# A decoder's second cross attention: where the layernorm behind its output projection is worked

## The chip, the cores and the metric

The kernel runs on 1 core of one Trainium2 chip. The metric is the time of one execution on the device in microseconds (us), less is better; three runs of the kernel before gave 1655.15, 1655.97 and 1658.78 us, median 1655.97.

## The reference

Two pre-norm decoder layers over x of 8 sequences x 112 tokens x 512, in float32. Each layer is self attention, cross attention to a context, and a feed-forward part:

```
x = x + _L1_xattn_ref(_layernorm(x, axis=-1), ctx_512, L1_xattn_Wq, L1_xattn_Wkv_expand, L1_xattn_Wout)
x = x + _L1_ffn_ref(_layernorm(x, axis=-1), L1_ffn_Wg, ..., L1_ffn_bsd)
```

The change lies between these two lines of the second layer. The cross attention has 16 heads of 32 with a causal mask over 112 keys, softmax, and the projection Wout (512 x 512). The layernorm that follows takes each token's mean and variance over 512 values, subtracts and divides by sqrt(var + 1e-5). The feed-forward part is a mixture of experts: two rounds, each with a gate, six routed experts and a shared part.

## The kernel before, in words

The program is written by hand: every stage has one function for each engine (pe_ for TensorE, act_ for ScalarE, dve_ for VectorE, pool_ for GpSimd), each engine works its list strictly in that order, and semaphores named by engine and step join them. So the order of the lines is the order of the work; there is no planner.

The 896 tokens (8 x 112) are held as NT = 7 tiles of 128 in x. A matrix product keeps float32 accuracy with three matmuls: each operand is split into a rounded high part and the rest, the low part (mm3, lines 261 to 263). For a normalised tile this is: transposing by TensorE into one PSUM bank in four pieces (ln_turn, line 266), a copy by ScalarE that rounds it, the high part (ln_hi, line 338), and a subtraction by VectorE, the low part (ln_lo, line 342).

pe_att2, act_att2, dve_att2 and pool_att2 are the cross attention, one sequence a wave, w from 0 to NB + 1 = 9. Wave w computes the scores of sequence w (banks 0 to 3), and turns and applies the probabilities of earlier ones: a sequence has two groups of heads, so group 15 is the last one. power is the exponential, sum8 and share8 the softmax's sum and division, turn8 and turned the transposing of the probabilities (banks 4, 5) and their copy, values the product with V (bank 6), hi and lo its high and low part (line 2002 and 2046). Bank 7 (FILL) takes what is done beside: from wave 5 to 8 the output tiles 0 to 3 (output2, 12 matmuls of 128x512), which dve_att2 adds to x (residual, line 768) and takes the statistics of (stats2, lines 2088 and 2090).

pe_o2, act_o2 and dve_o2 follow: output tiles 4, 5, 6, and the layernorm of all seven. root2 (line 2102) is the square root on ScalarE; norm2 the reciprocal (line 2095) and the scaling into RES (line 2097); RES lies over the keys K2. pe_o2 ends with a wait for the low part of tile 3, behind which pe_moe begins with up(0, 0): 24 matmuls of 128x448 that read tiles 0 to 3. Then it turns tile 6 (which waits for tile 4's low part), does the gate's products and goes on.

The weights come as a stream of pieces through three buffers stg: a DMA by SyncE, the rounding copy on ScalarE (round_w, line 302), the rest on GpSimd (rest_w, line 307). A buffer is loaded again once its rest is done. first_up is the first piece of the experts; the two behind it are copied in act_o2 behind tile 3's high part, and need that TensorE is done with output tile 6, whose weights lie in their place.

Of the kernel before, what the change touches and what calls it, by code (L numbers as in the profile page):

```python
# [14 lines left out]
NB, S, D, L = 8, 112, 512, 375  # L15
T = NB * S
P, NT = 128, NB * S // 128
# [58 lines left out]
def build(nc, g):  # L76
# [8 lines left out]
    with ExitStack() as ctx:  # L85
# [1812 lines left out]
        def pe_att2(e):  # L1898
            def scores(w):
                for i in range(4):  # L1900
                    if w:
                        e.wait_ge(*upon("act_a2", "exp", 2 * w - 2 + i // 2))
                    e.matmul(PS[0:S, i, 0:HT], one[0:S, 0:S], maskR[:, :].unsqueeze(1).to_broadcast([S, 4, S]), start=True,
                             stop=True)
                for c in range(4):
                    for i in range(4):
                        p = slice(32 * i, 32 * i + 32)
                        last = e.matmul(PS[0:S, i, c * S:(c + 1) * S], QO[p, 1 + 2 * w, c, :], K2[p, c, w * S:(w + 1) * S],
                                        start=False, stop=True, skip_group_check=True)
                        if c == 3:  # L1910
                            last.then_inc(*done("pe_a2", "sc", w, i))

            def less(u):
                e.wait_ge(*upon("dve_a2", "mx", u))
                for i in range(2):
                    last = e.matmul(PS[0:S, 2 * (u % 2) + i, 0:HT], one[0:S, 0:S], r4(nmr[:, u % 4, 4 * i:4 * i + 4], S),
                                    start=False, stop=True, skip_group_check=True)
                last.then_inc(*done("pe_a2", "sub", u))

            def values(w):  # L1920
                e.wait_ge(*upon("act_a2", "pt", 2 * w + 1))
                e.wait_ge(*(upon("dve_a2", "lo", w - 1) if w else upon("dve_ln", "ln2", NT - 1, "lo")))
                for c in range(4):
                    for i in range(4):
                        last = e.matmul(PS[32 * i:32 * i + 32, 6, c * S:(c + 1) * S],
                                        V2[:, w, 128 * c + 32 * i:128 * c + 32 * i + 32], PT[i // 2][:, 4 * (i % 2) + c, :],
                                        start=True, stop=True)
                last.then_inc(*done("pe_a2", "pv", w))

            def ahead(w):  # L1930
                if w < 4:
                    if w:
                        e.wait_ge(*upon("dve_q2", "v" if w == 3 else "k", *((2,) if w == 3 else (w - 1, 1))))
                    else:
                        e.wait_ge(*upon("act_q2", 1))
                        e.wait_ge(*upon("dve_ln", "ln2", NT - 1, "lo"))
                    query2(e, 4 + w, FILL)
                elif 4 < w < 9:
                    e.wait_ge(*upon("dve_q2", "v", w - 1))
                    output2(e, w - 5, FILL)  # L1940

            def between(w):
                if w < 4:
                    e.wait_ge(*upon("act_q2", 4 + w))
                    key2(e, w, 1, FILL)
                elif w == 4:
                    e.wait_ge(*upon("dve_q2", "v", 3))
                    value2(e, 4, FILL)
                elif w < 8:
                    e.wait_ge(*upon("dve_o2", "x", w - 5))  # L1950
                    value2(e, w, FILL)

            def behind(w):
                if w in (2, 3):
                    e.wait_ge(*upon("dve_q2", "k", w, 1))
                    value2(e, w, FILL)

            e.wait_ge(*upon("dve_q2", "v", 1))
            e.wait_ge(*upon("act_a2", "mask"))
            e.wait_ge(*upon("act_q2", 3))  # L1960
            for w in range(NB + 2):
                if w == 4:
                    e.wait_ge(*upon("act_q2", 7))
                    e.wait_ge(*upon("dve_q2", "k", 3, 1))
                if w < NB:
                    scores(w)
                if w > 1:
                    turn8(e, "a2", 2 * w - 3)
                ahead(w)
                if w < NB:  # L1970
                    less(2 * w)
                if w > 1:
                    e.wait_ge(*upon("dve_q2", "v", w - 2))
                    values(w - 2)
                between(w)
                if w < NB:
                    less(2 * w + 1)
                if 0 < w <= NB:
                    turn8(e, "a2", 2 * w - 2)
                behind(w)  # L1980
# [4 lines left out]
        def act_att2(e):  # L1985
            def power(u):
                if u > 3:
                    e.wait_ge(*upon("pe_a2", "tr", u - 4))
                e.wait_ge(*upon("pe_a2", "sub", u))
                e.activation(Sb[u % 4][:, :, :].rearrange("p (i j) s -> p i j s", i=2), pairv(2 * (u % 2)), ACT.Exp,  # L1990
                             scale=float(np.float32(1.0) / np.sqrt(np.float32(32.0)))).then_inc(*done("act_a2", "exp", u))

            def turned(u):
                if u > 1:
                    e.wait_ge(*upon("pe_a2", "pv", u // 2 - 1))
                e.wait_ge(*upon("pe_a2", "tr", u))
                e.activation(PT[u % 2][:, :, :].rearrange("p (i j) s -> p i j s", i=2), pairv(4),
                             ACT.Copy).then_inc(*done("act_a2", "pt", u))

            def hi(w):  # L2000
                e.wait_ge(*upon("pe_a2", "pv", w))
                e.activation(parts2(0, w), psv(6), ACT.Copy).then_inc(*done("act_a2", "hi", w))

            e.wait_ge(*upon("pe_ln", "ln2", NT - 1))
            e.activation(maskR[:, :], C("mask1", S), ACT.Copy).then_inc(*done("act_a2", "mask"))
            for w in range(NB + 2):
                if w > 1:
                    turned(2 * w - 3)
                if w < 4:
                    query2_out(e, 4 + w, FILL)  # L2010
                if w < NB:
                    power(2 * w)
                if w > 1:
                    hi(w - 2)
                if w < NB:
                    power(2 * w + 1)
                if 0 < w <= NB:
                    turned(2 * w - 2)
                if w in (2, 4):
                    round_w(e, piece["o2", w // 2 - 1][0])  # L2020
                if w == NB:
                    round_w(e, first_up)

        def dve_att2(e):
# [5 lines left out]
            for w in range(NB + 2):  # L2030
# [13 lines left out]
                if w > 1:  # L2044
                    e.wait_ge(*upon("act_a2", "hi", w - 2))
                    e.tensor_tensor(parts2(1, w - 2), psv(6), parts2(0, w - 2).bitcast(F),
                                    A.subtract).then_inc(*done("dve_a2", "lo", w - 2))
                if 4 < w < 9:
                    stats2(e, w - 5)
                if w < NB:  # L2050
                    sum8(e, "a2", 2 * w)
                if w in (2, 3):
# [51 lines left out]
        def pe_o2(e):  # L2104
            for t in range(4, NT):
# [1 line left out]
                if t == 4:  # L2107
                    e.wait_ge(*upon("act_a2", "pt", 2 * NB - 1))
                output2(e, t, t)
                if t > 4:  # L2110
                    ln_turn(e, "lne", t - 5, RES[:, t - 5, :], t - 5)
            for t in range(2, NT - 1):
                ln_turn(e, "lne", t, RES[:, t, :], t)
            e.wait_ge(*upon("dve_ln", "lne", 3, "lo"))

        def act_o2(e):
            for t in range(4):
                root2(e, t)
            root2(e, 4)
            ln_hi(e, "lne", 0, 0)  # L2120
            root2(e, 5)
            ln_hi(e, "lne", 1, 1)
            root2(e, 6)
            for t in range(2, NT - 1):
                ln_hi(e, "lne", t, t)
                if t == 3:
                    for k in (1, 2):
                        round_w(e, first_up + k)

        def dve_o2(e):  # L2130
            e.wait_ge(*upon("pe_a2", "sc", NB - 1, 3))
            norm2(e, 0)
            residual(e, "o2", 4)
            stats2(e, 4)
            norm2(e, 1)
            residual(e, "o2", 5)
            stats2(e, 5)
            ln_lo(e, "lne", 0, 0)
            norm2(e, 2)
            residual(e, "o2", 6)  # L2140
            stats2(e, 6)
            ln_lo(e, "lne", 1, 1)
            for t in range(3, NT):
                norm2(e, t)
                ln_lo(e, "lne", t - 1, t - 1)

        def pool_o2(e):
            for k in (1, 2):
# [649 lines left out]
```

## Time and profile before

| | |
|---|---|
| median of 3 runs | 1655.97 us |
| the profiled execution | 1654.79 us |
| its span | 1652.9 us |
| busy: PE, DVE, ACT, POOL | 96%, 57%, 44%, 40% |
| chain that ended last: PE, DVE, ACT, issue | 84%, 7%, 4%, 4% |
| mean granted TensorE clock | 0.992 |

A view of the profile lists instructions by start, duration, engine and source line; "idle before" is how long the engine had nothing, and the arrow says what ended it. The chain of waits is followed back from the last instruction of the program to what released each step. Times are us from the start of the span. The granted clock (PEclk) is a share of the full 2.4 GHz; 0.50 is 1.2 GHz. The execution's time is 1.89 us more than its span.

### The profile page before, as it was taken

To read this page: it belongs to the slowest core of one execution; us is meant where nothing else is said; L and a number is where in the kernel's file an instruction comes from. 1 tells how busy PE (TensorE), PEld (TensorE's weight loads), DVE (VectorE), ACT (ScalarE), POOL (GpSimd) and SP (SyncE) were. 2 spreads that over 40 slices of the span, in tenths; PEclk is the share of its full clock that TensorE was granted. 3 is DMA by queue.
4 is the path that set the end of the run, shared out by engine and by line. 5 is a ranking of instruction groups with operands and counts; after the bars stand their busy time and mean duration, and the time that the engine had idled before them with its cause. 6 is when DMAs were issued, how large, how long until landed. Compare 5 with 4: busy or idle time off the path is not lost.

```text
span 1652.9 us, 24562 instructions
## 1 busy us (share of the span) xinstructions
PE 1589.1 (96%) x9832; PEld 1353.0 (82%) x9832; DVE 939.1 (57%) x1531; ACT 733.0 (44%) x1231; POOL 665.8 (40%) x483
## 2 busy tenths in 40 slices
PE   7999999999999999989999989998989999999998
PEld 7998666778899998768889976877768888888887
DVE  6555663366545555687668566353766455554554
ACT  3113654322587765665511156333545334353342
POOL 3875542540498873421137633212422422222321
PEclk9999999999999999999999999999999999999999
DMA  4110003123222007200001100110011111111111
GB/s 166 52 64 28 2 2 121 50 85 128 93 88 64 14 2 266 93 1 1 1 13 64 52 26 2 48 39 26 20 33 39 45 64 45 51 46 51 51 58 45
DMA packets 28581, 88.52 MB, mean 54 GB/s; under 512 B 4155, under 2 KB 4283, under 8 KB 28216
## 3 DMA queue, kind: packets, MB, share of 16 engines
q1 hardware_dynamic: 28468, 86.96, 15.7%
q8 instruction: 79, 1.29, 0.3%
q14 instruction: 34, 0.27, 0.1%
HBM read 85.11 MB, written 1.84 MB: 53 GB/s over the span
## 4 chain that ended last, share of the span: by engine, by line
PE 84%; DVE 7%; ACT 4%; issue 4%; POOL 1%; DMA 0%; SPq 0%; ACTq 0%; DVEq 0%; POOLq 0%
PE PS L261 19%; PE PS L263 18%; PE PS L262 18%; PE PS L266 7%; PE PS L1125 4%; PE PS L1462 3%; PE PS L1477 2%; PE PS L561 2%; PE PS L952 1%; PE PS L585 1%; PE PS L1709 1%; PE PS L1697 1%; PE PS L551 1%; PE PS L569 1%; DVE xn L326 1%
## 5 line engine op out<-in xcount | busy, mean ns | idle before, releaser
L307 POOL TENSOR_TENSOR HL<-stg,HL 128x1024 fp32r<-128x1024 f32 (+2 forms) x111 | 243.9, 2200 | 515.8 <-ACT HL L302 497.7
L261 PE MATMUL PS<-XT,HL 128*128 128x448 f32 x608 | 226.1, 372 | 2.9 <-DVE XT L342 2.2
L263 PE MATMUL PS<-XT,HL 128*128 128x448 f32 x608 | 223.8, 368 | 0.0
L262 PE MATMUL PS<-XT,HL 128*128 128x448 f32 x608 | 223.7, 368 | 0.0
L302 ACT ACTIVATE HL<-stg 128x1024 fp32r<-128x1024 f32 (+2 forms) x111 | 104.5, 944 | 215.1 <-PE PS L263 199.1
L261 PE MATMUL PS<-HL,XT 128*128 128x512 f32 (+1 forms) x380 | 138.3, 364 | 2.0 <-POOL HL L307 1.2
L262 PE MATMUL PS<-HL,XT 128*128 128x512 f32 (+1 forms) x380 | 135.5, 356 | 0.0
L263 PE MATMUL PS<-HL,XT 128*128 128x512 f32 (+1 forms) x380 | 135.4, 356 | 0.0
L261 PEld LDWEIGHTS PS<-XT,HL 128*128 128x128 f32 x608 | 115.6, 190 | 15.2 <-DVE XT L342 3.3
L262 PEld LDWEIGHTS PS<-XT,HL 128*128 128x128 f32 x608 | 115.7, 190 | 9.3
L263 PEld LDWEIGHTS PS<-XT,HL 128*128 128x128 f32 x608 | 115.3, 190 | 9.4
L1076 POOL TENSOR_TENSOR Sx<-Sx,rx 112x750 f32<-112x750 f32 x64 | 91.8, 1440 | 54.0 <-DVE rx L1178 53.9
L2416 DVE SCALAR_TENSOR_TENSOR Hh<-PS,sml,Hh 128x448 fp32r<-128x448 f32 x64 | 43.8, 684 | 119.2 <-ACT Hh L2302 119.2
L261 PE MATMUL PS<-HL,Ph 128*128 128x512 f32 x224 | 90.4, 404 | 2.7 <-DVE ACC L2448 0.9
L725 DVE TENSOR_TENSOR XT<-QO,XT 128x896 fp32r<-128x896 f32 x32 | 36.8, 1159 | 98.4 <-ACT XT L719 98.4
L1738 POOL TENSOR_TENSOR Sb<-Sb,rc 112x896 f32<-112x896 f32 x32 | 53.7, 1685 | 94.3 <-DVE rc L1733 94.2
L2302 ACT ACTIVATE Hh<-PS,sml 128x448 fp32r<-128x448 f32 x64 | 40.6, 635 | 109.1 <-PE PS L263 109.1
L263 PE MATMUL PS<-HL,Ph 128*128 128x512 f32 x224 | 87.6, 391 | 0.0
L262 PE MATMUL PS<-HL,Ph 128*128 128x512 f32 x224 | 87.5, 391 | 0.0
L1125 PE MATMUL PS<-PX,kvr 125*128 125x224 f32 x384 | 84.2, 355 | 0.0
L261 PEld LDWEIGHTS PS<-HL,XT 128*128 128x128 f32 (+1 forms) x380 | 70.8, 186 | 14.1 <-issue 1.9
L1097 DVE TENSOR_REDUCE nm<-PS 112x2 f32<-112x750 f32 x64 | 60.1, 939 | 38.3 <-PE PS L263 38.3
(314 smaller groups left out, 3808.6 us busy)
## 6 DMA issues: line engine op xcount, KB each, us to landing
stg<-in_wst SPq DMA_DIRECT2D x87, 512.0 KB, 3.3
stg<-in_wst SPq DMA_DIRECT2D x16, 352.0 KB, 3.1
stg<-in_wst SPq DMA_DIRECT2D x16, 320.0 KB, 3.3
wsum<-in_wfc SPq DMA_DIRECT2D x8, 512.0 KB, 3.7
wsum<-in_wpj SPq DMA_DIRECT2D x8, 512.0 KB, 3.5
raw<-in_wfc SPq DMA_DIRECT2D x8, 512.0 KB, 7.5
stg<-in_wst SPq DMA_DIRECT2D x16, 256.0 KB, 2.7
raw<-in_wpj SPq DMA_DIRECT2D x7, 512.0 KB, 7.0
```

The source lines that it names most:

```text
L261: e.matmul(out, lh, rh, start=start, stop=False)
L262: e.matmul(out, lh, rl, start=False, stop=False)
L263: return e.matmul(out, ll, rh, start=False, stop=stop)
L266: return e.transpose(out, in_, C("ident", n)[:, 0:n])
L302: e.activation(slot(k)[:, 0, 0:n], stg[k % NSTG][:, 0:n], ACT.Copy).then_inc(*done("act_w", k))
L307: e.tensor_tensor(slot(k)[:, 1, 0:n], stg[k % NSTG][:, 0:n], slot(k)[:, 0, 0:n].bitcast(F), A.subtract).then_inc(*done("pool_w", k))
L1076: e.tensor_tensor(Sx[k][:, :, :], Sx[k][:, :, :], rx[:, k, :].unsqueeze(2).to_broadcast([S, 2, L]), A.mult).then_inc(*done("pool_x", "p", u))
L1097: e.tensor_reduce(nm[:, u % 4, :], PS[0:S, bank:bank + 2, 0:L], AX.X, A.max, negate=True).then_inc(*done("dve_x", "nm", u))
L1125: last = e.matmul(PS[:, 6 + u % 2, 0:2 * S], kvr[:, c, u // 8, :], PX[u % 2][:, :, c, :], start=c == 0, stop=c == 2)
L1462: last = e.matmul(PS[:, 7, :], YT[c4][:, hl, kc, :], w_rows(ter, 1, c4 * 4 + kc), start=c4 == 0 and kc == 0 and hl == 0, stop=c4 == 3 and ...
L1738: e.tensor_tensor(Sb[k][:, :, :], Sb[k][:, :, :], b8(rc[:, k, :]), A.mult).then_inc(*done(f"pool_{tag}", "p", u))
L2416: e.scalar_tensor_tensor(out=half_of(Hh[:, 1, ch, :], h), in0=PS[:, 2 * h + ch, 0:HT], scalar=M("bup")[:, 2 * n + ch:2 * n + ch + 1], in1= ...
```

## The change

```diff
 pe_att2, wave w
                 if w > 1:
                     turn8(e, "a2", 2 * w - 3)
+                if w > NB:
+                    for t in range(2):
+                        ln_turn(e, "lne", t, RES[:, t, :], t)
                 ahead(w)
...
 act_att2, wave w
                 if w > 1:
                     turned(2 * w - 3)
+                if w == NB:
+                    for t in range(3):
+                        root2(e, t)
+                elif w > NB:
+                    ln_hi(e, "lne", 0, 0)
...
                 if w == NB:
+                    root2(e, 3)
                     round_w(e, first_up)
...
 dve_att2, wave w, behind the low part of sequence w - 2
+                if w == NB:
+                    norm2(e, 0)
+                    norm2(e, 1)
                 if 4 < w < 9:
                     stats2(e, w - 5)
+                if w == NB:
+                    norm2(e, 2)
...
 pe_o2
                 output2(e, t, t)
-                if t > 4:
-                    ln_turn(e, "lne", t - 5, RES[:, t - 5, :], t - 5)
+                ln_turn(e, "lne", t - 2, RES[:, t - 2, :], t - 2)
+            ln_turn(e, "lne", 5, RES[:, 5, :], 5)
+            e.wait_ge(*upon("dve_ln", "lne", 3, "lo"))
+
+        def act_o2(e):
+            ln_hi(e, "lne", 1, 1)
             for t in range(2, NT - 1):
-                ln_turn(e, "lne", t, RES[:, t, :], t)
-            e.wait_ge(*upon("dve_ln", "lne", 3, "lo"))
-
-        def act_o2(e):
-            for t in range(4):
-                root2(e, t)
-            root2(e, 4)
-            ln_hi(e, "lne", 0, 0)
-            root2(e, 5)
-            ln_hi(e, "lne", 1, 1)
-            root2(e, 6)
-            for t in range(2, NT - 1):
+                if t < 5:
+                    root2(e, t + 2)
                 ln_hi(e, "lne", t, t)
                 if t == 3:
                     for k in (1, 2):
                         round_w(e, first_up + k)
 
         def dve_o2(e):
-            e.wait_ge(*upon("pe_a2", "sc", NB - 1, 3))
-            norm2(e, 0)
-            residual(e, "o2", 4)
-            stats2(e, 4)
-            norm2(e, 1)
-            residual(e, "o2", 5)
-            stats2(e, 5)
             ln_lo(e, "lne", 0, 0)
-            norm2(e, 2)
-            residual(e, "o2", 6)
-            stats2(e, 6)
+            norm2(e, 3)
             ln_lo(e, "lne", 1, 1)
-            for t in range(3, NT):
+            for t in range(4, NT):
+                residual(e, "o2", t)
+                stats2(e, t)
+                ln_lo(e, "lne", t - 2, t - 2)
                 norm2(e, t)
-                ln_lo(e, "lne", t - 1, t - 1)
+            ln_lo(e, "lne", 5, 5)
```

No instruction is added or taken away; they change place. On VectorE the layernorm of tiles 0 to 2 moves into wave 8, and from tile 4 on each tile is worked as residual, statistics, low part of the tile two behind, scaling.

## Rows read from the trace of the kernel before

**Rows 1.** The page: busy time, share of the span and instructions by engine.
```profile
PE 1589.1 (96%) x9832; PEld 1353.0 (82%) x9832; DVE 939.1 (57%) x1531; ACT 733.0 (44%) x1231; POOL 665.8 (40%) x483
```
**Rows 2.** Stretches: length, busy time by engine, granted clock, DMA share, GB/s.
```profile
1204.20:1216.00 11.80, 8.34 (x104) 6.74 (x105) 5.54 (x12) 6.09 (x9) 5.68 (x3) 1.00 0.00 1
...
1224.20:1231.20 7.00, 2.74 (x19) 2.02 (x18) 6.66 (x15) 3.92 (x7) 2.35 (x2) 0.87 0.01 3
1231.20:1236.20 5.00, 5.00 (x15) 4.45 (x14) 2.31 (x2) 0.71 (x2) 1.42 (x1) 0.50 0.66 207
1236.20:1240.60 4.40, 4.40 (x32) 2.72 (x30) 1.96 (x3) 1.64 (x3) 0.00 (x0) 1.00 0.02 4
```
**Rows 3.** The chain of waits, 1213 to 1237 us: start, us, engine, tile, line.
```profile
1213.04 1.11 issue
...
1224.04 0.70 DVE x L768
...
1227.65 0.61 ACT XT L338
...
1230.45 1.11 PE PS L266 x4
1231.57 0.37 PE PS L261
...
1236.79 0.20 PE PS L261
```
**Rows 4.** Instructions of PE: start, us, engine, line, operation, out<-in, count.
```profile
1212.09 0.95 PE L266 MATMUL PS<-cst,Sb 112*112 112x112 f32 x8 [1.16 <-ACT PT L1997]
...
1215.06 0.50 PE L261 MATMUL PS<-HL,XT 128*128 128x512 f32 x1
...
1223.84 1.03 PE L266 MATMUL PS<-cst,RES 128*128 128x128 f32 x8
```
**Rows 5.** Instructions of ACT, 1206 to 1223 us.
```profile
1206.43 0.92 ACT L1997 ACTIVATE PT<-PS 112x896 f32<-112x896 f32 x1 [1.19 <-PE PS L266]
1210.09 0.55 ACT L2002 ACTIVATE XT<-PS 128x448 fp32r<-128x448 f32 x1 [2.73 <-PE PS L1925]
...
1211.84 1.05 ACT L302 ACTIVATE HL<-stg 128x1024 fp32r<-128x1024 f32 x1
...
1215.75 1.28 ACT L2102 ACT_TABLE_LOAD   x1
1217.04 0.85 ACT L2102 ACTIVATE qs<-qs,eps 128x1 f32<-128x1 f32 x4
...
1222.50 0.29 ACT L2102 ACTIVATE rs<-mv,eps 128x1 f32<-128x1 f32 x1 [0.64 <-DVE mv L2090]
```
**Rows 6.** Instructions of DVE, 1211 to 1223 us.
```profile
1211.28 0.68 DVE L2088 BATCH_NORM_STATS2 qs<-x 128x6 f32<-128x512 f32 x1
...
1222.29 0.18 DVE L2090 BATCH_NORM_AGGREGATE mv<-st 128x2 f32<-128x6 f32 x1
1222.39 0.66 DVE L342 TENSOR_TENSOR XT<-PS,XT 128x512 fp32r<-128x512 f32 x1
1222.96 0.15 DVE L2095 RECIPROCAL qs<-qs 128x1 f32<-128x1 f32 x1
```
**Rows 7.** Line 2097: durations in ns (min/median/max), first and last start.
```profile
L2097 DVE TENSOR_SCALAR RES<-x,qs x4: 545/546/547, 1217.6 to 1226.4; 128x512 f32<-128x512 f32 x4
L2097 DVE TENSOR_SCALAR RES<-x,mv,rs x2: 545/931/1317, 1227.6 to 1229.1; 128x512 f32<-128x512 f32 x2
L2097 DVE TENSOR_SCALAR RES<-x,mvl,rsl x1: 1801/1801/1801, 1231.1 to 1231.1; 128x512 f32<-128x512 f32 x1
```
**Rows 8.** Instructions of POOL, 1228 to 1233 us.
```profile
1228.85 3.77 POOL L307 TENSOR_TENSOR HL<-stg,HL 128x512 fp32r<-128x512 f32 x2 [13.53 <-ACT HL L302]
```
**Rows 9.** Instructions of PE, 339 to 342 us: a pause in another stage.
```profile
340.99 0.85 PE L869 MATMUL PS<-stg 128*128 128x64 f32 x6 [1.67 <-ACT Cf L899]
```
**Rows 10.** The stretch behind that pause.
```profile
342.00:345.30 3.30, 3.30 (x9) 2.52 (x8) 0.41 (x1) 0.00 (x0) 3.14 (x5) 0.50 0.36 109
```

## The prediction, made before the changed kernel was run

> **What bounds the kernel now.** Read first the busy line of the page [rows 1]: TensorE works 96% of the span, so only what lets it pause, or slows its clock, can be won back. Next come the stretches around the change [rows 2]. From 1224.2 to 1231.2 TensorE is busy 2.74 of 7.00 us while VectorE is busy 6.66: the layernorm's tail is a VectorE stretch. In the 5 us behind it TensorE is busy throughout but at 0.50 of its clock, and in the next stretch at 1.00 again. So this boundary costs twice, by the pause and by the slow clock after it. The chain of waits [rows 3] says who holds it: output tile 6 ends at 1224.04, the chain goes over VectorE's residual, ScalarE's high part at 1227.65 and VectorE again, and comes back to TensorE only at 1230.45 for the turn of tile 5; up(0, 0) starts at 1231.57. Last, each engine's list in order of time [rows 4 to 8], for durations and for what each step would stand behind.
>
> **Wave 8, ScalarE.** turned(13) runs from 1206.43 to 1207.35, and hi(6) starts at 1210.09 after 2.73 us of idling [rows 5]. The table load (1.28) and three roots now fall in here: four took 0.85, with 0.28 to 0.30 for one alone, so three take about 0.65. They end near 1209.3, 0.8 us before hi(6). I cost them at nothing; if that cover were gone, each us would delay hi(6) and all below by one. The load starts 0.02 us after the copy in front of it has ended and the first root the moment it ends (1215.75 + 1.28 against 1217.04 [rows 5]), so the trace shows no price beyond the 1.28. The Trainium skill, "ScalarE: Activation LUTs", section "What ACT_TABLE_LOAD costs", adds a drain of about 1.38 us to the load. By that rule the roots would end near 1210.65 and everything behind be 0.55 us late.
>
> **Wave 8, VectorE.** Before, tile 3's statistics start at 1211.28 [rows 6], right behind the low part. Now two norm2 stand in front. One is a reciprocal of 0.15 [rows 6] and a scaling of 0.55 [rows 7], about 0.65 from start to start since neighbours overlap a little (bounds: 0.55, and 0.70 without overlap). Statistics start at 1212.6 and their aggregate is done 0.9 later, at 1213.5. The third norm2 ends at 1214.2, before lo(7) needs VectorE (1215.76 before): hidden.
>
> **Wave 8, ScalarE again: the price of the change.** root2(3) waits for that aggregate, and behind it are queued the copy of piece first_up (1.05 us, at 1211.84 before [rows 5]), then turned(15), for which TensorE's values(7) waits, and hi(7). The root costs 0.2 to the next start: the copy starts at 1213.7, 1.9 later than before. turned(15) began at 1213.13, 0.24 after that copy's end, when TensorE had turned group 15 (1212.09 + 0.95 [rows 4]); now it begins at the copy's end, 1214.7, and values(7) starts at 1215.7 instead of 1214.15 (the end of the 1.11 in [rows 3]): 1.55 late. Bounds: 1.3 (norm2 at 0.55) and 1.8. Into the longer pause fall the turns of tiles 0 and 1, which took 1.03 together [rows 4] and stood between and behind output tiles 5 and 6. They fit, but about 1.65 us of pause stay in one piece. The stream loses nothing: piece first_up has its rest near 1217.3, ten us before up(0, 0), and the DMA that waits for that rest brings a piece first copied behind up(0, 0).
>
> **The output tiles.** With everything from values(7) on shifted by 1.55, output tile 4 ends near 1219.65 (before about 1218.1: 1215.13, from the first matmul [rows 4], plus 12 x 0.23 and the start). One turn of 0.44 stands behind each tile: 5 ends near 1222.9, 6 near 1226.1, against 1224.04 before [rows 3].
> VectorE: lo(7) at 1217.35, then ln_lo(0), norm2(3), ln_lo(1) at 0.55, 0.6, 0.65, 0.6 start to start: residual(4) at 1219.7, just as tile 4 is done. From there VectorE sets the pace. A tile is residual 0.7 [rows 3] and statistics 0.7 [rows 6], 0.03 each to start; aggregate 0.18; root 0.03 + 0.2 to the next start (the root at 1222.50 follows the aggregate of 1222.29 + 0.18 [rows 5, 6]); high part 0.61 [rows 3], 0.08 to VectorE; low part 0.58, norm2 0.65. Sum 3.77. VectorE stands still for about 1 us of it, because the low part of the tile two behind has its high part queued behind this tile's root. TensorE needs 3.2 a tile, so it isn't the limit. residual(5) at 1223.5, ln_lo(3) at 1226.0, norm2(5) at 1226.6, scaled at 1227.35. TensorE turns tile 4 at 1226.1 without a wait, pauses 0.8 us, and turns tile 5 at 1227.4; ln_lo(3) is done before. up(0, 0) starts at 1227.9 against 1231.57: 3.7 us earlier (bounds 3.0 and 4.2, by the bounds above and 0.2 of rounding a tile).
> Tile 6: two weight copies stand before its root on ScalarE, root at 1228.9, RES at 1231.1, low parts of 4 and 5 by 1231.7. up(0, 0) covers it until 1232.8.
>
> **The clock.** Of up(0, 0)'s matmuls those from 1231.57 to 1236.2 ran at half clock, 0.37 from one to the next against 0.20 after [rows 2, 3]: 4.65 x (1 - 0.20/0.37) = 2.1 us lost. Before it TensorE idled 4.3 of 7 us. With single pauses of 0.8 us I take the clock to stay at 2.4 GHz and all of it to come back (bounds 0 and 2.3).
>
> **POOL.** norm2's scaling took 545 ns five times, but 1317 and 1801 in the two whose starts (1229.1, 1231.1) lie inside GpSimd's two weight rests, 1228.85 to 1232.6 [rows 7, 8]. Those rests follow the two copies, now released by tile 6's end at 1226.1, so GpSimd starts near 1226.85, and tile 5's scaling, which TensorE waits for, at 1226.8. A tie within my accuracy: 0 to 1.25 us, nearest to the 0.77 of the first such row; half of it, 0.4.
>
> **Sum.** -3.7 - 2.1 + 0.4 = -5.4 us. On the profiled execution 1654.79 - 5.4 = 1649.4; that one stands 1.2 under the median, and on the median 1655.97 it is 1650.6. What follows up(0, 0) is released by TensorE itself and moves along.
>
> **The rivals.**
> A. The clock falls in the new pause. A single pause of 1.67 us was followed by 3.3 us at 0.50 elsewhere [rows 9, 10], and mine is 1.65. Against it: 3.46 us of idling in three pieces from 1204.2 to 1216 left the clock at 1.00 [rows 2]. Price 3.3 x 0.46 = 1.5 on output tiles 4 and 5, passed on since VectorE waits for tile 4: 1652.1. Chance 0.25.
> B. The rests overtake the scaling: +0.8 to 1.25 instead of 0.4, and the pause before tile 5's turn grows to 1.6 to 2.1, after which the clock may be low for up(0, 0) as it was (2.1). 1651.0 to 1653.5, say 1652.3. Chance 0.14.
> C. The table load with its drain: +0.55, 1651.2. Chance 0.04.
> D. The experts are held elsewhere, by weights or by VectorE's work on the gate, and the gain is given back: 1655 to 1656. In the trace those waits follow TensorE's own steps. Chance 0.04.
> E. Slower. Idling in wave 8 and 9 brings the clock down at 1215.7 and it stays down, since each turned and output step is followed by another wait. An us at half clock costs 0.46, so the 3.3 won by order (3.7 - 0.4) are gone at 7.2 us of it beside the present 4.65; from about 11.8 in all the kernel is slower. If 1215.7 to 1236 were slow throughout, 20.3 us, that is 7.2 lost beside what is lost now, and 3.9 slower: 1659.9. Against it: after other pauses full clock returned while TensorE was busy [rows 2]. Chance 0.04.
> F. GpSimd comes late: 1650.2 or a little under, the forecast's other side. Chance 0.05.
>
> **Chances and range.** The forecast has 0.44, the rest as given. 0.2% (3.3 us) is what a measurement tells from no change. The forecast, F and C, most of A and over half of B lie below 1652.7: 0.82 faster; D, the rest of A and B: 0.14 the same; E: 0.04. The range 1648.8 to 1653.4 takes in A, most of B and the better bounds (4.2 + 2.3 from the median is 1649.5, and the lowest run lies 0.8 under the median).
>
> **What would show it.** In the changed trace: the table load near 1207.4 and hi(6) still at 1210.1; values(7) about 1.5 late; up(0, 0) near 1227.9 with 0.20 us a matmul and granted clock 1.00; the scaling of tile 5 at 545 ns or over 1300. It is wrong if values(7) is over 2 late, if the clock is under 1.00 in 1215 to 1223 or behind 1227, or if VectorE's round of a tile takes over 4 us.

## The result, and the profile after

The changed kernel takes 1647.40 us (median of 8 runs, 1646.96 to 1653.43) against 1656.05 (8 runs, 1654.62 to 1660.36); ratio 0.9948, 95% interval 0.9935 to 0.9962. Forecast were 1650.6 and 1648.8 to 1653.4: the right way, but 8.65 us won where 5.4 were forecast, and the time is below the range. The profiled execution took 1647.46, its span is 1645.7.

The stretches that answer to [rows 2] (length, busy PE, PEld, DVE, ACT, POOL, granted clock, DMA share, GB/s):

```profile
1202.80:1214.60 11.80, 7.69 (x91) 6.38 (x95) 7.15 (x17) 7.86 (x13) 4.48 (x3) 1.00 0.00 0
1214.60:1225.00 10.40, 10.40 (x76) 8.36 (x67) 7.22 (x15) 2.95 (x8) 1.21 (x1) 1.00 0.08 27
1225.00:1232.00 7.00, 6.16 (x37) 5.44 (x40) 4.83 (x11) 3.75 (x8) 3.94 (x2) 1.00 0.45 150
```

The seven us in which TensorE was busy 2.74 are gone, and none of the three stretches is under 1.00. TensorE's list, for [rows 4] and the turns of [rows 3]:

```profile
1204.00 0.95 PE L266 MATMUL PS<-cst,Sb 112*112 112x112 f32 x8 [1.20 <-ACT PT L2000]
...
1210.69 0.95 PE L266 MATMUL PS<-cst,Sb 112*112 112x112 f32 x8 [1.16 <-ACT PT L2000]
1211.48 1.04 PE L266 MATMUL PS<-cst,RES 128*128 128x128 f32 x8
1214.27 0.97 PE L1925 MATMUL PS<-PT,V 112*32 112x112 f32 x32 [1.75 <-issue]
...
1225.88 0.66 PE L266 MATMUL PS<-cst,RES 128*128 128x128 f32 x4 [0.84 <-DVE RES L2111]
1226.29 0.45 PE L261 MATMUL PS<-XT,HL 128*128 128x448 f32 x1
...
1231.24 0.60 PE L266 MATMUL PS<-cst,RES 128*128 128x128 f32 x4
1231.77 1.69 PE L2238 MATMUL PS<-XT,sml 128*8 128x448 f32 x16
```

One ruler serves for everything below: **the stretch** from the turn of group 13 (here 1204.00) to the gate's products (here 1231.77). The same two ends in the kernel before, with the first matmul of up(0, 0) between them:

```profile
1205.38 0.95 PE L266 MATMUL PS<-cst,Sb 112*112 112x112 f32 x8 [1.20 <-ACT PT L1997]
...
1231.22 0.72 PE L261 MATMUL PS<-XT,HL 128*128 128x448 f32 x1
...
1238.98 1.69 PE L2236 MATMUL PS<-XT,sml 128*8 128x448 f32 x16
```

The stretch is 27.77 us here and was 33.60. What follows it is 413.9 us in both, so nothing is given back. The other 1.4 us between the two spans lie ahead of the stretch, where the kernels are the same: the trace of before shows the clock at 0.50 from 342 to 345.3 [rows 10], and in the changed one it is full there:

```profile
342.00:345.30 3.30, 3.30 (x19) 2.73 (x18) 1.66 (x4) 0.00 (x0) 3.14 (x5) 1.00 0.34 114
```

19 matmuls instead of 9 in the same time, after the same pause of 1.67 us. Over all 16 traces here TensorE's clock falls at nine places of this program, at most of them in some executions only. Two executions of the changed kernel in its third set, of 1780 and 8896 us, stand far outside all others and are left out below; no run shows their cause.

ScalarE, for [rows 5], and the scaling of tile 5 with GpSimd's rests, for [rows 7, 8]:

```profile
1205.99 1.28 ACT L2116 ACT_TABLE_LOAD   x1
1207.28 0.67 ACT L2116 ACTIVATE qs<-qs,eps 128x1 f32<-128x1 f32 x3
1208.69 0.54 ACT L2005 ACTIVATE XT<-PS 128x448 fp32r<-128x448 f32 x1 [0.74 <-PE PS L1925]
...
1212.12 0.29 ACT L2116 ACTIVATE qs<-qs,eps 128x1 f32<-128x1 f32 x1 [1.58 <-DVE qs L2109]
1212.33 1.04 ACT L302 ACTIVATE HL<-stg 128x1024 fp32r<-128x1024 f32 x1
1213.27 0.90 ACT L2000 ACTIVATE PT<-PS 112x896 f32<-112x896 f32 x1
```
```profile
1225.28 0.55 DVE L2111 TENSOR_SCALAR RES<-x,mv,rs 128x512 f32<-128x512 f32 x1
```
```profile
1225.41 3.94 POOL L307 TENSOR_TENSOR HL<-stg,HL 128x512 fp32r<-128x512 f32 x2 [9.60 <-ACT HL L302]
```

### The profile page after: what moved, and what is told of

Same layout as the page of the kernel before. It is cut to its first block, busy times and chain, and to the rows that moved or that the text cites. A ratio compares the mean times of both kernels' runs of the same rounds, so it can differ in the third digit from the quotient of the medians.

```text
span 1645.7 us, 24561 instructions
## 1 busy us (share of the span) xinstructions
PE 1584.0 (96%) x9832; PEld 1347.7 (82%) x9832; DVE 937.4 (57%) x1531; ACT 732.5 (45%) x1231; POOL 665.3 (40%) x483
## 4 chain that ended last, share of the span: by engine, by line
PE 84%; DVE 7%; ACT 4%; issue 4%; POOL 1%; ACTq 0%; DVEq 0%; POOLq 0%
PE PS L261 19%; PE PS L263 18%; PE PS L262 18%; PE PS L266 7%; PE PS L1125 4%; PE PS L1462 3%; PE PS L1477 2%; PE PS L561 2%; PE PS L952 1%; PE PS L585 1%; PE PS L1709 1%; PE PS L1697 1%; PE PS L551 1%; PE PS L569 1%; DVE xn L326 1%
```

## The experiments

Theory 1: the change is worth what its order does in the stretch, plus a clock loss of the kernel before that differs between executions and that one trace showed too small. Rivals: the falls are a property of the kernel; or something behind the stretch gained. "Won" and every ratio are against the kernel before, timed beside that variant.

**The kernel before and the changed one again.** No edit.

> The kernel before, unchanged, timed against itself: what a ratio is worth here, and a second trace of it. Theory 1 (the change is worth the 5.8 us that the two traces show between the turn of group 13 and the turn of tile 6; the other 1.4 us between the two spans, and the rest of the 8.65 between the medians, are falls of TensorE's clock that come and go between executions of the same code): the median is within 1.5 us of the other runs of before, the clock's falls stand at other places than in the first trace, and what happens between 1224 and 1237 costs another amount, up to 3.5 us of slow clock instead of 2.1. Theory 2 (the falls are the same in every execution of one kernel): the trace has the same falls as the first, at 40, 341, 741, 1117 and 1229 us.

> The changed kernel, unchanged, a second trace. Theory 1: ratio 0.995 with 6 to 9 us won; in this trace too the clock is 1.00 from wave 8 to the experts, and up(0, 0) starts within 0.1 us of where it did, counted from the turn of group 13 (22.3 us); the falls elsewhere differ from the first trace, which had none at 40 and 341. Theory 2: no falls at 40 and 341 again.

> The kernel before, a third trace. How much does slow clock cost between the turn of group 13 and the gate's products in another execution? Two traces have 33.6 and 35.3 us for this stretch, where the changed kernel has 27.8 in both. Theory 1: the pause around 1227 always brings the clock down, at a time that differs, so 33.3 to 35.5, and a fall in wave 9 in some. Theory 2 (2.1 us is the rule, the second trace an exception): 33.6 within 0.2.

> The kernel before, a fourth trace, with the same two theories as before_look1: 33.3 to 35.5 us for the stretch by theory 1, 33.6 within 0.2 by theory 2.

> The kernel before, a fifth trace, with the same two theories as before_look1: 33.3 to 35.5 us for the stretch by theory 1, 33.6 within 0.2 by theory 2.

> The changed kernel, a third trace and more times. In the kernel before the clock fell in waves 8 and 9 in 4 of 5 traces (1.5 us each), in the changed kernel in neither of 2, nor in 4 variants of it that keep the two turns there. Theory 1 (the two turns between the pauses keep it up): 27.8 us again from the turn of group 13 to the gate's products, clock 1.00. Rival (chance; the longer pause of 1.75 us brings it down in part of the executions): 29.3 or more here.

Against itself the kernel before gave 0.9998 (0.9988 to 1.0009). The changed one gave 0.9961 (0.9948 to 0.9973) and 0.9963 (0.9949 to 0.9976). The stretch in the five traces of before: 33.60, 35.26, 33.83, 35.13, 35.30, mean 34.6; in the three of the changed kernel: 27.77, 27.75, 27.77. The part behind it is 413.7 to 414.0 in all eight, so the rival behind the stretch is out. Ahead of it the kernels are equal on the mean: the turn of group 13 stands at 1204.9 in the five and at 1205.0 in the three. Theory 1 is borne out, but not where it looked: behind up(0, 0) the slow clock cost 2.3 us in the first trace and 2.4, 1.0, 2.4 and 2.5 in the others. What is new lies in wave 9 and the first matmuls of output tile 4, at a low clock in four of the five; the trace I had forecast from was the exception. The seven us from 1211 to 1218 in the first trace, and in before_again, look1, look2 and look3:

```profile
1211.00:1218.00 7.00, 4.80 (x53) 3.98 (x54) 2.29 (x6) 5.46 (x9) 2.35 (x1) 1.00 0.13 40
```
```profile
1211.00:1218.00 7.00, 5.53 (x49) 4.52 (x50) 1.55 (x5) 4.76 (x9) 2.35 (x1) 0.76 0.13 40
```
```profile
1211.00:1218.00 7.00, 5.89 (x51) 4.65 (x50) 1.33 (x3) 4.11 (x8) 2.35 (x1) 0.76 0.14 40
```
```profile
1211.00:1218.00 7.00, 5.15 (x48) 4.20 (x49) 1.58 (x5) 4.85 (x8) 2.35 (x1) 0.76 0.15 40
```
```profile
1211.00:1218.00 7.00, 5.10 (x47) 4.17 (x48) 1.58 (x5) 4.85 (x8) 2.35 (x1) 0.76 0.14 40
```

The work is the same; the clock is 1.00 in one and 0.76 in four. In the four, up(0, 0) starts 27.3 to 27.4 us after the turn of group 13 instead of 25.84: 1.5 us.

**The clock without the order.** filled puts matmuls that compute nothing needed into the kernel before, in the pauses ahead of the turns of tiles 3, 4 and 5; filled_all also ahead of the turns of groups 13 and 15 and of the last values, five in each pause. The edit of filled:

```diff
+            e.wait_ge(*upon("dve_o2", "x", 3))
             for t in range(2, NT - 1):
+                for _ in range((0, 8, 2, 6)[t - 2]):
+                    e.matmul(PS[0:S, FILL, 0:HT], one[0:S, 0:S], maskR[:, :].unsqueeze(1).to_broadcast([S, 4, S]), start=True,
+                             stop=True)
                 ln_turn(e, "lne", t, RES[:, t, :], t)
```

> The kernel before with 16 extra matmuls of 112x448 (0.19 us each) in TensorE's pauses ahead of the turns of tiles 3, 4 and 5; nothing else moves. It parts the clock from the pause: up(0, 0) should start where it did, 0 to 0.4 us later, with the clock at 1.00. Theory 1: the traced boundary is 2.1 us shorter, the median 2 to 3.5 us lower (1652.5 to 1654). A rival: the clock is worth less, since fillers delay the turns and VectorE's work is the limit: 0 to 1 us. If the clock falls in spite of the fillers: no change.

> filled with 5 matmuls of 112x448 more in each of TensorE's three pauses in waves 8 and 9 (1.20, 1.16 and 1.11 us before the turns of groups 13 and 15 and before the last values). In the second trace of the kernel before the clock fell there (1212 to 1217) and cost 1.6 us that my sum had not. Theory 1 (that happens in part of the executions of before and of filled, and is one share of what the medians show beyond the trace): the median is 0 to 1.5 us under filled's 1653.3, and the slowest runs go. Rival (the fall in waves 8 and 9 is rare): the same as filled, or up to 0.3 us worse by fillers that end late.

filled: 1653.31 us, 1.8 won, ratio 0.9986 (0.9972 to 1.0), less than the 2 to 3.5 expected and at the edge of noise. filled_all: 1650.82, 4.1 won, 0.9978 (0.9968 to 0.9987). That is 2.5 under filled by the medians, more than the 0 to 1.5 expected, and 1.8 by the means. Their traces, from 1218 to 1236:

```profile
1218.00:1236.00 18.00, 16.97 (x91) 13.96 (x90) 14.61 (x28) 6.61 (x13) 3.83 (x2) 1.00 0.18 60
```
```profile
1218.00:1236.00 18.00, 16.96 (x100) 13.52 (x102) 14.23 (x28) 7.48 (x14) 3.84 (x2) 1.00 0.18 60
```

The clock is 1.00 and the stretch 30.95 and 31.01 us. So of the 6.9 us that the change wins in the mean stretch (34.6 against 27.8), 3.6 are clock alone and 3.2 the order. In wave 9, where filled is still the kernel before, its trace has full clock too:

```profile
1211.00:1218.00 7.00, 5.09 (x54) 4.24 (x55) 2.30 (x7) 5.19 (x9) 2.35 (x1) 1.00 0.14 40
```

So the fall in wave 9 came in four of six traces of that code. That filled_all wins more than filled fits a fall in wave 9 in part of filled's other executions.

**The turns out of the pause.** turns_back takes the turns of tiles 0 and 1 out of wave 9, and tile 0's high part (not shown) behind the last hi:

```diff
-                if w > NB:
-                    for t in range(2):
-                        ln_turn(e, "lne", t, RES[:, t, :], t)
...
+                if t == 4:
+                    for i in range(2):
+                        ln_turn(e, "lne", i, RES[:, i, :], i)
                 output2(e, t, t)
```

> The changed kernel with the turns of tiles 0 and 1 taken out of wave 9's pause and put ahead of output tile 4, behind values(7), and tile 0's high part behind hi(7). Undoes one part. Theory 1 (in the pause they are free, outside they cost what they take): values(7) starts where it did, output tile 4 is 0.8 us later, and VectorE, which waits for it, passes that on: 0.8 us worse than the changed kernel. The pause grows from 1.75 to 2.7 us in one piece, and in some executions the clock falls there: a median 0.8 to 2.5 us worse. Rival (the clock doesn't care): 0.8 and not more.

1651.42 us, ratio 0.9974 (0.9963 to 0.9985). PE in its trace, and the 6.3 us from inside the pause on:

```profile
1214.86 0.95 PE L266 MATMUL PS<-cst,Sb 112*112 112x112 f32 x8 [1.16 <-ACT PT L1997]
1218.43 1.72 PE L1925 MATMUL PS<-PT,V 112*32 112x112 f32 x32 [2.62 <-issue]
```
```profile
1217.00:1223.30 6.30, 4.87 (x44) 4.28 (x45) 2.03 (x5) 3.07 (x5) 2.35 (x1) 0.50 0.14 44
```

The pause is 2.62 in one piece and the clock 0.50 for 6.3 us from 1217.0, of which TensorE works 4.87: the stretch is 30.97, 3.2 more, of which 0.8 is the turns' own time (forecast) and the other 2.4 the clock. The times agree: the median is 3.8 over the changed kernel's 27 undisturbed runs (1647.61), the mean 3.2 (1651.90 against 1648.73). So the two turns are worth more as filling than as work done early. This pause is longer than any in wave 9 of the kernel before, so it shows what the turns do in the changed kernel, not why the shorter pauses of the kernel before bring the clock down.

**The price in wave 8.** stats_first works tile 3's statistics ahead of the scalings; copies_late also moves two weight copies.

```diff
-                if w == NB:
-                    norm2(e, 0)
-                    norm2(e, 1)
                 if 4 < w < 9:
                     stats2(e, w - 5)
                 if w == NB:
-                    norm2(e, 2)
+                    for t in range(3):
+                        norm2(e, t)
... copies_late, act_o2
-                if t == 3:
+                if t == 5:
                     for k in (1, 2):
                         round_w(e, first_up + k)
```

> The changed kernel with tile 3's statistics ahead of the scaling of tiles 0 to 2 in wave 8. It takes away the price I put on the change: root2(3), the weight copy and turned(15) come 1.3 us earlier, so values(7) starts 0.3 us instead of 1.55 us later than before, and the turns of tiles 0 and 1 still lie in the pause. Theory 1: 1.3 us less than the changed kernel (1646.1), all of it at values(7) and passed on, since VectorE waits for output tile 4. Rival (VectorE's round of 3.77 us a tile is the limit whatever comes before): 0 to 0.3 us.

> stats_first with the copies of the second and third weight piece behind tile 5's high part instead of tile 3's, so that GpSimd's rests start about 3 us later. In stats_first the scaling of tile 5 began within 0.01 us of GpSimd's rest, took 1.56 instead of 0.55 us, TensorE stood 1.97 us before tile 5's turn and the clock fell: that gave back the 1.34 us won at values(7). Theory 1 (the collision is the cause): the scaling of tile 5 takes 0.55 again, up(0, 0) starts 21.0 us after the turn of group 13 (22.1 in stats_first, 22.3 in the changed kernel), clock 1.00, median 1 to 1.5 us under the changed kernel's. Rival (the scaling is slow for another reason, or VectorE's round is the limit): it stays over 1 us and nothing is won.

stats_first: 1650.09, ratio 0.9963 (0.9952 to 0.9975), no gain on the changed kernel (0.9961, timed beside it), and a stretch of 29.14, 1.4 longer. Neither theory had the cause. values(7) starts 8.93 after the turn of group 13 instead of 10.27, the 1.34 expected; but look at VectorE, then GpSimd, then TensorE:

```profile
1215.00 2.62 DVE L2109 TENSOR_SCALAR RES<-x,qs 128x512 f32<-128x512 f32 x1
...
1226.93 1.56 DVE L2109 TENSOR_SCALAR RES<-x,mv,rs 128x512 f32<-128x512 f32 x1
```
```profile
1214.96 2.38 POOL L307 TENSOR_TENSOR HL<-stg,HL 128x1024 fp32r<-128x1024 f32 x1 [3.76 <-ACT HL L302]
1226.94 3.78 POOL L307 TENSOR_TENSOR HL<-stg,HL 128x512 fp32r<-128x512 f32 x2 [9.60 <-ACT HL L302]
```
```profile
1228.55 0.66 PE L266 MATMUL PS<-cst,RES 128*128 128x128 f32 x4 [1.97 <-DVE RES L2109]
```
```profile
1229.20:1232.60 3.40, 3.40 (x11) 3.00 (x10) 2.48 (x6) 1.27 (x3) 1.53 (x1) 0.50 0.71 227
```

Tile 5's scaling meets GpSimd's rest to within 0.01 us and takes 1.56 instead of 0.55; TensorE waits 1.97, and the clock falls, which costs 1.6 us between up(0, 0) and the gate's products (7.04 against 5.48). This is rival B of the prediction, brought about by coming earlier. copies_late takes the meeting away: the pause is 0.96, the scaling 0.55, up(0, 0) at 21.1 and the stretch 26.55, 1.2 under the changed kernel's. Its time, 1648.16 us, 0.9950 (0.9938 to 0.9962), is from only 5 runs and doesn't show the 1 to 1.5 us expected.

```profile
1223.65 0.55 DVE L2109 TENSOR_SCALAR RES<-x,mv,rs 128x512 f32<-128x512 f32 x1
```

**VectorE's round.** hi_first swaps ScalarE's root and high part; both adds stats_first's edit.

```diff
-                if t < 5:
-                    root2(e, t + 2)
                 ln_hi(e, "lne", t, t)
+                if t < 5:
+                    root2(e, t + 2)
```

> The changed kernel with each high part ahead of the root on ScalarE (tile t before the root of tile t + 2). It takes away the wait of 0.85 us that VectorE's low part has behind each tile's statistics. Theory 1: VectorE's round falls from 3.73 us to 2.9, TensorE with 3.2 becomes the limit, tile 5 is scaled before output tile 6 ends, the pause of 0.84 us before its turn goes, and up(0, 0) starts 21.3 us after the turn of group 13 instead of 22.3: 1.0 us won. The scaling of tile 5 is then also clear of GpSimd. Rival (the root is now late and norm2 waits for it): 0 to 0.4 us won.

> stats_first and hi_first together. Theory 1: 1.3 + 1.0 = 2.4 us under the changed kernel, up(0, 0) 19.9 to 20.0 us after the turn of group 13; tile 2's scaling still takes 2.6 us beside GpSimd's first rest, at a cost of 0.1 us. Rival: TensorE is the limit from output tile 4 on in either, so the two don't add: 1.3 us.

> both once more, beside the changed kernel on one chip, since their medians (1646.84 of 5 runs against 1647.6 of 17) lie closer than the 2.40 us between their traced stretches. Theory 1: 25.4 us for the stretch again, and a median 2.4 us under the changed kernel's; the clock's falls elsewhere, which differ from one execution to the next, hid it. Rival: the 2.4 us are given back further on, and the part of the span behind the stretch is longer than 413.9 us.

hi_first: the stretch is 26.72 and up(0, 0) starts at 21.25, 1.04 earlier. VectorE in it:

```profile
1223.88 0.68 DVE L768 TENSOR_TENSOR x<-PS,x 128x512 f32<-128x512 f32 x1
...
1225.32 0.18 DVE L2104 BATCH_NORM_AGGREGATE mv<-st 128x2 f32<-128x6 f32 x1
1225.41 0.66 DVE L342 TENSOR_TENSOR XT<-PS,XT 128x512 fp32r<-128x512 f32 x1
...
1227.05 0.69 DVE L768 TENSOR_TENSOR x<-PS,x 128x512 f32<-128x512 f32 x1 [0.32 <-PE PS L263]
```

The low part follows the aggregate at once, and now VectorE waits for TensorE. 1647.92 us from 5 runs, 0.9949 (0.9935 to 0.9962): the 1.0 us is seen in the stretch and not in the times. both: the two add, 25.37 and 25.41 in its traces, 2.4 under the changed kernel, with TensorE never idle in the 17 us from the last values on:

```profile
1215.00:1232.00 17.00, 17.00 (x120) 14.20 (x124) 15.12 (x27) 7.47 (x15) 5.17 (x3) 1.00 0.20 67
```

Medians 1646.84 and 1646.19, ratios 0.9944 (0.9932 to 0.9957) and 0.9947 (0.9931 to 0.9963): the best of all, but its 11 runs have a median 0.9 and a mean 1.9 under the 27 of the changed kernel (1646.73 and 1646.85 against 1647.61 and 1648.73). Giving back is not the reason: what follows the stretch is 413.9 and 414.2. Falls of the clock elsewhere scatter both by more than that; that they hid the rest is argued, not shown.

## Why the prediction missed

What it said of the changed kernel came out: each of the signs that it had named in the changed trace is there. What it had wrong is the kernel before. Step by step, with the turn of group 13 as zero (1205.38 before, 1204.00 after):

- Table load at nothing: right. hi(6) waited 0.74 us for TensorE behind the roots (0.8 forecast). The load starts 0.02 us behind the copy in front of it and the roots follow the load without a gap (1205.99 + 1.28 to 1207.28), so rival C is out. The Trainium skill, "ScalarE: Activation LUTs", section "What ACT_TABLE_LOAD costs", gives a drain of about 1.38 us beside the load; the trace does not agree, and the measurement decides.
- values(7) 1.55 late: it came at 10.27 against 8.77, 1.50 late. stats_first shows the cause, by 1.34.
- Output tiles, VectorE's round of 3.77: 3.73 (residuals at 1218.27, 1222.01, 1225.74). up(0, 0)'s first matmul 22.29 against 25.84: 3.55 (3.7 forecast). Of this 0.35 is clock, since tile 5's turn was slow before: in filled up(0, 0) starts at 25.49. The order itself is 3.2.
- POOL at 0.4: 0, the scaling came 0.13 us ahead of GpSimd. Step mis-sized by 0.4, but the race is real, as stats_first shows.
- **The clock at 2.1: the failed step, mis-sized.** Between the two first traces it is right: 5.83 us in the stretch, 3.55 + 2.3. But the term was read from one execution, and that it fits there is the luck of two traces. On the mean over five, the kernel before loses 3.6 to the clock in the stretch: 2.1 behind up(0, 0), 0.35 in tile 5's turn, and 1.5 in wave 9 in four of five, which is 1.2. I took the one trace's clock of 1.00 in 1204.2 to 1216 [rows 2] for what always happens, used it as the argument against rival A, and gave that rival to the changed kernel alone. It was the other way round: it is the kernel before that falls there, and the changed one did in none of three traces. Nor did the four variants that keep the turns in wave 9 (hi_first with the same pauses, the other three with shorter ones); stats_first's fall comes later. That the turns hold the clock by splitting the idling rests on turns_back, one trace and seven times.
- The sum: the mean stretch is 6.9 us shorter, 3.6 by the clock (2.1 forecast) and 3.2 by the order (3.3 forecast, 3.7 - 0.4). The means of all undisturbed runs, 1655.76 (100 runs) and 1648.73 (27), differ by 7.0. The medians, 1655.53 and 1647.61, differ by 7.9 and those of the first eight runs of each by 8.65. Of the 3.25 between that and the forecast, 1.5 are the clock term; the 1.8 beyond 6.9 stand in no stretch of the traces. I take them for which falls elsewhere the few runs drew; that isn't shown.

Open: why a pause of given length brings the clock down in one execution and not in the next.

## What to carry to other kernels

Where TensorE pauses, take the clock's cost from several traces of the unchanged kernel, not from one; a single trace shows one draw. Two short turns put into a pause can be worth more by holding the clock than by being done early; where nothing useful is at hand, matmuls that compute nothing can do it (4.1 us here). After making a stretch faster, look whether a scaling on VectorE now meets work on GpSimd.

## What the runs showed of the hardware

- A scaling (tensor_scalar, SBUF to SBUF, float32) that begins while GpSimd works waits for that instruction: it ended 0.28 us after it in stats_first (1215.00 + 2.62 against 1214.96 + 2.38), 2.62 us instead of 0.55. Begun 0.13 us ahead of GpSimd it took its 0.55. The Trainium skill, "SBUF — State Buffer", section "SBUF: two separate sides", says of a VectorE instruction in a two-port mode and a GpSimd instruction that whichever starts first holds the shared pair of ports for its whole instruction, and the other is blocked. The traces agree in who waits and for how long; the mode of this scaling no run shows. In stats_first's second meeting the records put the scaling 0.01 us ahead and it waited all the same, so who is first can't be read from them that closely. Low parts and residuals, which read PSUM, took 0.6 to 0.7 us beside GpSimd as elsewhere.
- Behind pauses of 1.20, 1.16 and 1.11 us with matmuls between them the clock went to 0.50 in 4 of 5 traces of the kernel before and stayed at 1.00 in the fifth and in filled, for the same instructions. At half clock the last values took 1.72 us (before_again) and at full clock 0.97 (filled):

```profile
1213.42 1.72 PE L1925 MATMUL PS<-PT,V 112*32 112x112 f32 x32 [1.11 <-issue]
```
```profile
1213.86 0.97 PE L1925 MATMUL PS<-PT,V 112*32 112x112 f32 x32 [1.11 <-issue]
```
